# A four-direction scan: two of the four products move from GpSimd to VectorE, in a new order

## What is computed

```python
def _s6(x, ...):                       # x: (batch, sequence, 24), latent width 64
    u = x @ xw.T + xb
    Bm, Cm = split(x @ bcw.T + bcb)
    A_bar = exp(-softplus(delta))      # delta = x @ dw.T + db; this is sigmoid(-delta)
    elems = (A_bar, (1.0 - A_bar) * Bm * u)
    h = scan(elems)                    # h[t] = A_bar[t] * h[t-1] + B_bar[t] * u[t]
    return _linear(Cm * h, yw, yb)
s1 = x by rows; s2 = x by columns; s3 = s1 reversed; s4 = s2 reversed
y_cat = concatenate([_s6(s) for s in (s1, s2, s3, s4)])
out = _linear(_linear(y_cat, mw, mb) * sigmoid(_linear(y_cat, gw, gb)), ow, ob)
```

## Time and profile before

| what | value |
|---|---|
| median of 3 runs | 3313.1 us (3307.01 to 3316.84) |
| the profiled execution | 3312.04 us, span 3310.4 us |
| mean granted TensorE clock | 0.969 |
| busy: PE, DVE, ACT, POOL | 2831.6, 2666.6, 2258.8, 1860.7 us |
| scans of the phase, L2150 (row groups, column groups) | 153.0 us and 196.8 us in the groups of 112 |
| GpSimd's products, L2209 | 263.7 us in 192, 104.9 us in 64 |

### The profile page before, as it was taken

How to read it: one execution, slowest core, us unless ns; L and a number is a source line. 1 busy time by engine, 2 the same in 40 slices (tenths; PEclk the granted TensorE clock), 3 DMA queues, 4 the chain that set the end, 5 groups by cost and what they waited for, 6 DMA issues and landing times. The chain is left out here.

```text
span 3310.4 us, 65685 instructions
## 1 busy us (share of the span) xinstructions
PE 2831.6 (86%) x20846; PEld 1477.4 (45%) x20846; DVE 2666.6 (81%) x4380; ACT 2258.8 (68%) x4205; POOL 1860.7 (56%) x1466
## 2 busy tenths in 40 slices
PE   8999989686999999999997678789999779688876
PEld 5666654233444444444442224344444334477732
DVE  6888879536999999999999958769999968444468
ACT  5666658576999898989895427666777558444455
POOL 2333323155889898989897635447777745100046
PEclk9999999898999999999999999989999989899999
DMA  2000001256474747474746232201101012301023
GB/s 88 0 0 0 0 14 45 81 172 175 120 209 135 221 140 222 140 217 141 217 124 185 59 79 74 76 21 25 24 23 25 18 56 89 126 22 23 22 71 78
DMA packets 201533, 294.28 MB, mean 89 GB/s; under 512 B 62242, under 2 KB 179158, under 8 KB 201110
## 3 DMA queue, kind: packets, MB, share of 16 engines
q1 hardware_dynamic: 198678, 288.03, 30.3%
q10 hardware_dynamic: 2688, 4.29, 0.4%
HBM read 190.11 MB, written 102.09 MB: 88 GB/s over the span
## 5 line engine op out<-in xcount | busy, mean ns | idle before, releaser
L1780 POOL TENSOR_TENSOR mam_hc<-mam_h,mam_cs 128x896 f32<-128x896 f32 x336 | 703.5, 2094 | 173.5 <-DVE mam_h L1699 98.7
L1699 DVE TENSOR_TENSOR_SCAN mam_h<-mam_a,mam_kept,mam_dbx 128x448 f32<-128x448 f32 x672 | 737.7, 1127 | 48.4 <-ACT mam_a L1569 47.4
L1422 PE MATMUL mam_ps_y<-mam_hc,mam_ident 128*128 128x448 f32 x1344 | 570.8, 558 | 124.8 <-POOL mam_hc L1780 124.7
L1569 ACT ACTIVATE mam_a<-mam_ft,mam_a_neg 128x448 f32<-128x448 f32 x672 | 409.5, 657 | 77.1 <-DVE mam_h L1699 76.0
L1422 PEld LDWEIGHTS mam_ps_y<-mam_hc,mam_ident 128*128 128x128 f32 x1344 | 249.8, 193 | 425.4 <-POOL mam_hc L1780 216.2
L1686 DVE TENSOR_TENSOR mam_dbx<-mam_ps_u,mam_bs 128x448 f32<-128x448 f32 x672 | 380.7, 610 | 0.0
L682 POOL TENSOR_TENSOR att_prob<-att_prob,att_share 128x588 f32<-128x588 f32 x128 | 149.0, 1186 | 306.8 <-DVE att_share L974 306.8
L2209 POOL TENSOR_TENSOR scan_ch<-scan_h,scan_cs 128x392 f32<-128x392 f32 x192 | 263.7, 1387 | 56.5 <-DVE scan_h L2150 55.3
L368 POOL MEMSET f_squares_ln<- 128x392 f32 x4 | 1.7, 424 | 362.5 <-POOLq L2283 326.5
L387 POOL CAST f_h<-f_hr 128x392 fp8e5<-128x392 f16 x128 | 65.3, 510 | 234.1 <-DVE f_hr L308 234.1
L2150 DVE TENSOR_TENSOR_SCAN scan_h<-scan_decay_by_column,scan_h,scan_drive_by_column 128x392 f32<-128x392 f32 x112 | 196.8, 1757 | 0.0
(11 more groups left out here) (240 smaller groups left out, 6631.1 us busy)
## 6 DMA issues: line engine op xcount, KB each, us to landing
mam_taps<-normed SPq DMA_DIRECT2D x220, 130.5 KB
mam_bs<-dram_bc SPq DMA_DIRECT2D x56, 448.0 KB, 9.1
mam_cs<-dram_bc SPq DMA_DIRECT2D x56, 448.0 KB, 11.7
normed<-f_staged SPq DMA_DIRECT2D x96, 203.0 KB
mam_ft<-dram_steps SPq DMA_DIRECT2D x42, 448.0 KB, 4.8
f_mixed<-mixed SPq DMA_DIRECT2D x64, 196.0 KB, 2.4
mam_gt<-dram_gs SPq DMA_DIRECT2D x48, 224.0 KB, 2.7
dram_gs<-mam_gs SPq DMA_DIRECT2D x47, 224.0 KB, 2.8
```

The source lines that it names most:

```text
L1422: mm = pe.matmul(ps_y[p % 2][:, 0:MT], ident[:], hc[t % 2][:, i, :], start=False, stop=(t % 8 == 7 and i == 1))
L1569: act.activation(a[t % 3][:, i, :], ft[p % 2][:, 0, :], ACT.Exp, scale=a_neg[:, at:at + 1]).then_inc(decays, 1)
L1699: dve.tensor_tensor_scan(h[:, n % 8, :], a[t % 3][:, i, :], dbx[:, i, 0:MT], kept[:, at:at + 1], ALU.mult, ALU.add).then_inc(scanned, 1)
L1780: pool.tensor_tensor(hc[t % 2][:], h[:, row:row + 2, :], cs[:, 2 * pair:2 * pair + 2, :], ALU.mult).then_inc(weighed, 1)
```

## The change

In VectorE's slot the products of the two column directions are added (`weigh_columns`, twice), and the order becomes: scans 0 and 1, `share`, `tail`, scans 2 and 3, `drive_with`, the two column products. GpSimd keeps the two row products and waits for both row scans before the first. The counter `weighed` becomes two, `weighed_rows` and `weighed_columns`, and all that waited for it waits for both or for the one of the product it reads. VectorE's wait for `sided` at the start of a slot is for one count more, since it now reads `cs`.

```diff
@@ tensor
-                        pe.wait_ge(weighed, done(c - 1, DIRS) + (n + 1))
+                        pe.wait_ge(weighed_rows if n < 2 else weighed_columns,
+                                   done(c - 1, 2) + (n % 2 + 1))
@@ scalar
-                            act.wait_ge(weighed, done((f - 1) * K - 1, DIRS))
+                            act.wait_ge(weighed_rows, done((f - 1) * K - 1, 2))
+                            act.wait_ge(weighed_columns, done((f - 1) * K - 1, 2))
@@ vector
+                def weigh_columns(c, half, k, p, n):
+                    d = ORDER[n]
+                    dve.wait_ge(scanned, done(c - 1, DIRS) + (n + 1))
+                    dve.wait_ge(merged, done(c - 1))
+                    hd = h[p][:, n, :].rearrange("p (x y) -> p x y", y=SIDE)
+                    out = products(n, p)[:, :]
+                    if d not in FORWARD:
+                        out = out[:, ::-1]
+                    out = out.rearrange("p (x y) -> p x y", y=SIDE)
+                    dve.tensor_tensor(out, hd, in_order(cs, half, d, k), ALU.mult
+                                      ).then_inc(weighed_columns, 1)
+
                 def slot(f, b, half, k, p, has_tail, j):
                     if b is not None:
                         c = b * K + k
                         dve.wait_ge(fronted, done(b * K + (K - 1)))
-                        dve.wait_ge(sided, done(b * K + (K - 1), 4) - 1)
+                        dve.wait_ge(sided, done(b * K + (K - 1), 4))
                         dve.wait_ge(scanned, done(c - 1, DIRS))
-                        dve.wait_ge(weighed, done(c - 2, DIRS))
-                        for n in range(3):
-                            if n == 2:
-                                dve.wait_ge(turned, done(b * K + (K - 1)))
-                            scan(c, 1 - half, k, p, n)
+                        dve.wait_ge(weighed_rows, done(c - 2, 2))
+                        dve.wait_ge(weighed_columns, done(c - 2, 2))
+                        scan(c, 1 - half, k, p, 0)
+                        scan(c, 1 - half, k, p, 1)
+                    if f is not None:
+                        share(f, k, p)
+                    if f is not None and b is None:
+                        drive_with(f, half, k, p)
                     if has_tail:
                         tail(b * K + k - 1, 1 - p)
-                    if f is not None:
-                        share(f, k, p)
                     if b is not None:
+                        dve.wait_ge(turned, done(b * K + (K - 1)))
+                        scan(c, 1 - half, k, p, 2)
                         scan(c, 1 - half, k, p, 3)
-                    if f is not None:
-                        drive_with(f, half, k, p)
+                        if f is not None:
+                            drive_with(f, half, k, p)
+                        weigh_columns(c, 1 - half, k, p, 2)
+                        weigh_columns(c, 1 - half, k, p, 3)
@@ gpsimd
-                    for n, d in enumerate(ORDER):
-                        pool.wait_ge(scanned, done(c - 1, DIRS) + (n + 1))
+                    pool.wait_ge(scanned, done(c - 1, DIRS) + 2)
+                    for n in range(2):
+                        d = ORDER[n]
                         if n == 1:
                             pool.wait_ge(merged, done(c - 1))
...
-                        pool.tensor_tensor(out, hd, in_order(cs, 1 - half, d, k), ALU.mult
-                                           ).then_inc(weighed, 1)
+                        pool.tensor_tensor(out, h[p][:, n, :], in_order(cs, 1 - half, d, k), ALU.mult
+                                           ).then_inc(weighed_rows, 1)
```

More of the change, by code:

```diff
@@ L1893, in four_scan_phase @@
         left, opened = buf.sem("left"), buf.sem("opened")
[L1894 to L1897, removed]
+        (projected, sided, multiplied, fronted, turned, scanned, weighed_rows, weighed_columns,
+         merged, sigmoided, gated, outed, resulted) = (buf.sem(n) for n in (
+             "projected", "sided", "multiplied", "fronted", "turned", "scanned", "weighed_rows",
+             "weighed_columns", "merged", "sigmoided", "gated", "outed", "resulted"))
         U, DELTA, B_, C_ = range(4)
         counters = ((projected, 4), (sided, 4), (multiplied, 1), (fronted, 1), (turned, 1),
-                    (scanned, DIRS), (weighed, DIRS), (merged, 1), (gated, 1), (outed, 1))
+                    (scanned, DIRS), (weighed_rows, 2), (weighed_columns, 2),
+                    (merged, 1), (gated, 1), (outed, 1))
         def done(c, per_chunk=1):
@@ L2197, in slot @@
                     pool.wait_ge(sided, done(b * K + (K - 1), 4))
-                    for n, d in enumerate(ORDER):
-                        pool.wait_ge(scanned, done(c - 1, DIRS) + (n + 1))
+                    pool.wait_ge(scanned, done(c - 1, DIRS) + 2)
+                    for n in range(2):
+                        d = ORDER[n]
                         if n == 1:
                             pool.wait_ge(merged, done(c - 1))
-                        hd, out = h[p][:, n, :], products(n, p)[:, :]
+                        out = products(n, p)[:, :]
                         if d not in FORWARD:
                             out = out[:, ::-1]
-                        if d not in BY_ROW:
-                            hd = hd.rearrange("p (x y) -> p x y", y=SIDE)
-                            out = out.rearrange("p (x y) -> p x y", y=SIDE)
-                        pool.tensor_tensor(out, hd, in_order(cs, 1 - half, d, k), ALU.mult
-                                           ).then_inc(weighed, 1)
+                        pool.tensor_tensor(out, h[p][:, n, :], in_order(cs, 1 - half, d, k), ALU.mult
+                                           ).then_inc(weighed_rows, 1)
                 stages(pool, slot, lambda c, p: None)
```

## The result

| | before | changed |
|---|---|---|
| median | 3314.6 us (4 runs) | 3369.01 us (4 runs, 3367.78 to 3376.84) |
| ratio | | 1.0173, 95% interval 1.015 to 1.0196 |
| profiled execution, span | 3312.04, 3310.4 | 3368.8, 3367.2 |
| start of the first full slot's first scan, of the last stage's | 2187.56, 2606.76 | 2189.87, 2662.58 |
| one full slot, the difference over 56 | 7.486 | 8.441 |

1.7% slower; forecast 3373. Of the 56.8 us between the spans, 56 x 0.955 = 53.5 are in the full slots. The first scan of the first full slot started 2.3 us later, with nothing changed in the layers ahead of the phase.

A forecast was written before the change was run, and what follows sets the result against it. VectorE's queue was taken to bound the kernel; after the change, a circle of waits would. +58.4 us in 56 full slots and +2.3 in the last stage, +61 on 3312.0, gave 3373 us, range 3320 to 3395.

The forecast's parts named there:

- VectorE sets the pace before: In full slots of 7.486 us, VectorE's queue bounds the kernel; its scans lose 2.4 us a slot to GpSimd.
- Who comes second waits: VectorE's scans and GpSimd's products seem to run one at a time, stretching scans from 1.00 to as much as 1.90 us.
- Scans of 0.92 us to the next: On VectorE, four scans free of GpSimd take 0.92 us each to the next instruction, 3.68 a slot.
- The column product at 0.99 us: On VectorE, a product of 392 elements stepping 224 bytes takes 0.99 us, 0.91 to the next; lower end 0.566.
- GpSimd's row products undisturbed at 0.8 us: GpSimd's row products take some 0.8 us each and end about 1.9 us after r1, so c2 loses nothing.
- The circle: Second column product through TensorE and ScalarE to `share`, 3.35 us, plus 5.18 us of VectorE work: 8.53 us a slot.
- Sum: The full slot's circle of waits totals 8.53 us against 7.49 before, +1.04 a slot, +58.4 us over 56 slots.
- Last stage +2.3 us: The last 8 slots, without projections, go from 7.21 to 7.5 us, taking low clock half and half: +2.3 us.
- Rival 1: The step costs VectorE nothing in the column products, 0.566 us each; slot 7.79 us, total 3327 us; chance 0.22.
- Rival 2: VectorE's freed time counts: its 6.94 us of work a slot sets the pace, total 3281 us; chance 0.07.
- Rival 3: TensorE's clock falls to 1.2 GHz in the column merges: circle 0.75 us longer, +42 us, total 3415; chance 0.08.
- Rival 4: The change evens out, c2 or TensorE being a little quicker: within 10 us of the time before; chance 0.08.

The follow-up runs named there:

- x9: The kernel before with GpSimd's four products cut to one element each, waits and order unchanged; 3256.4 us, ratio 0.9837.
- x3: The changed kernel with both column products reading `cs` contiguously (other pixels, same amount of work); 3339.6 us, ratio 1.007.
- x1: The changed kernel with VectorE's order of before, the two column products standing last, behind `drive_with`; 3310.5 us, ratio 0.9994.
- x5: The changed kernel with `drive_with` moved behind the two column products; 3360.6 us, ratio 1.0146.
- x7: The kernel before with the two row products on VectorE, right behind the row scans, and the column products left on GpSimd; 3293.6 us, ratio 0.9948.

## Why the prediction was right

Forecast 3373, measured 3369.0, inside the range of 3320 to 3395. The mechanism is the one forecast. That the number is within 4 us is in part luck: the full slots added 53.5 us and not 58.4, the last stage 0.15 and not 2.3, and 2.3 us came from ahead of the phase, where nothing was changed. By its steps:

- *VectorE sets the pace before, and loses 2.4 us a slot to GpSimd.* Right: x9's scans take 1.02 us each. "Who comes second waits" was read off four durations and holds to 0.02 us in x9. The Trainium skill says the same of this pair ("SBUF — State Buffer", SBUF: two separate sides: an exclusive lock between a VectorE instruction with two inputs from SBUF and a GpSimd instruction that reads SBUF); the trace agrees.
- *Scans of 0.92 us to the next.* 1.87 for the two between tail and `drive_with`: +0.03 us a slot.
- *The column product at 0.99 us, 0.91 to the next.* It took 0.876 and 0.79, nearer to the upper end than to the lower (0.566; x3 measured 0.557). The step is charged, but VectorE pays 0.32 us for it and not the 0.42 that ScalarE's rows suggested. GpSimd pays 0.20 (1.01 to 1.21), so the second support of the 0.42 was wrong. -0.23 us a slot. Of the two pages of the Trainium skill that were weighed, "SBUF — State Buffer" (Specifications, lines of 16 bytes) agrees with the 0.876 against 0.557; "VectorE: DVE Perf Modes" (Mode 1×), taken as one result a cycle at odd strides too, does not, and the measurement decides.
- *GpSimd's row products undisturbed at 0.8 us.* They take 1.01. The 0.8 was read from the end of a scan to the end of the product that had waited for it, and about 0.2 us of an instruction pass during such a wait: in the earlier trace rows scan c2, too, ends 0.82 us behind the product that held it up (2407.68 to 2408.50), and alone takes 1.02. This changed nothing: the second ended at 2404.59, and the scan c2 started at 2405.09. With 0.5 us less room it would have.
- *The circle: 1.04 to the gate, 2.27 to the end of `rest`, 0.04 to `share`.* 1.03, 2.28, 0.12.
- *Sum:* 8.53 forecast, 8.44 measured, over the 56 slots and in the one of the timeline: -0.23 in the products, +0.08 on the way to `share`, +0.06 in scans, tail and `drive_with`.
- *Last stage +2.3 us.* From the first scan to the last product it was +0.15. The slots were sized well (7.45 us measured between the first scans, 7.5 forecast, 7.21 before), but the sum took eight of them for the whole stage: the last product now ends 7.45 us after the last slot's first scan, and before it ended 8.99 us after it. Half and half for the low clock was a guess; from 2660 to 2725 us the granted clock was 0.92.

Rival 1 (the step costs nothing) is what x3 makes real: 3339.6, slot 7.96, where its sum gave 7.79. The way from the product to `share` was 3.61 us (3.47 forecast), the rest 0.05 longer in the slot of its timeline. Rival 2 (VectorE's freed time counts) fails by 1.56 us of idle time in every slot; x1 shows that the same split with the circle's way covered gives 3310.5, not 3281, since GpSimd then holds up c3 by 0.5 us and ScalarE is ready only just in time. Rival 3 (the clock): the middle slots held 1.00. Rival 4 (the change evens out): the time lies 54 us above the kernel before.

What I didn't see is that the circle has a fourth member in waiting. ScalarE had 1.67 us between the end of `turn` and the gate activation; x5 moves `drive_with`, and `turn` with it, about 2.05 us back, which is 0.4 too much, and I had counted `turn` at nothing there.

## What to carry to other kernels

In a software pipeline over several engines an order is good when what an engine makes last in a slot isn't what it needs first in the next. Before moving work to the engine that has none to spare, follow the result of its last instruction round the other engines back to it, and compare that time with the work that stands between; here 3.4 us of way met 1.9 us of work. When all engines get idle time and the time gets longer, look for such a circle and test it by moving one cheap call out of it. Of two kinds of work to hand over, hand over the one that is cheap on the taker: here contiguous rows (0.47 us) and not strided columns (0.80 us).

## What the runs showed of the hardware

A read with a step of 224 bytes in one of two operands adds 0.32 us to VectorE's product of 392 elements (0.557 to 0.876) and 0.20 to GpSimd's (1.01 to 1.21, x7 against the changed kernel). A scan of 392 elements takes 1.02 us, 1.8 times the contiguous product's 0.557. GpSimd waits for the end of a scan even for a product of one element (0.83 us instead of 0.19, x9). Some 0.2 us of an instruction pass during such a wait: in the kernel before, a scan and a product that had been held up ended 0.83 and 0.81 us after the other engine was done (medians of the middle slots), where alone they take 1.02 and 1.01.
